# First chunk of an embedding tower: rows of eight fields by one-hot products from whole tables instead of gathers

## Chip, cores, metric

The kernel runs on one core of one Trainium2 chip. The metric is the device time of one execution, in microseconds. All arithmetic is in float32.

## What is computed

A batch of 512 rows has 32 id fields. Each id picks a row of 64 numbers from its field's table. For each of the 496 pairs of fields, a 64x64 matrix stands between the two rows, and each pair gives one number. These 496 numbers and 16 dense ones go through three dense layers.

```python
e = jnp.stack([tbl_0[ids[:, 0]], ..., tbl_31[ids[:, 31]]], axis=1)   # 512 x 32 x 64
p, q = e[:, ids_x, :], e[:, ids_y, :]                                # all pairs x < y, 496
z = einsum('bpj,bpj->bp', einsum('bpi,pij->bpj', p, w), q)           # w: 496 x 64 x 64
h = jnp.concatenate([z, dense_ctx], axis=1)                          # 512 x 512
h = jnp.maximum(h @ W_top1 + b_top1, 0.0)                            # 512
h = jnp.maximum(h @ W_top2 + b_top2, 0.0)                            # 256
y = h @ W_top3                                                       # 512 x 1
```

Twelve of the tables have 1,000 rows; the others have 1,250, 12,500 or 125,000.

## The kernel before

The batch is cut into four chunks of 128 rows. GpSimd gathers, chunk by chunk and field by field, 128 rows of 64 numbers into `emb` (L313). Two neighbouring fields make a pair `k` of 128 numbers; TensorE turns a pair over by products with `identity` (L491) into a slot of `pu`, and ScalarE copies it to `eT` (L332), where the 128 numbers are partitions and the batch rows are columns. Chunk 0 is turned pair by pair (`XN[0]` is 1), later chunks four pairs at a time.

The pair products of a chunk are 32 units. A unit is 1024 columns of `pu`, two banks of 512. There are two ways to make one.

- A **turned** unit (16 of 32, list `TURNED`) has batch rows as partitions: two products of 512 columns (L523), one for each half of the 128 rows of `eT` and `ws`. VectorE multiplies it with `emb` into `turned` (L425). Then each of its 16 numbers for each batch row is a sum over 64, a row sum. A block of 16 row sums is made by ScalarE (16 instructions, L342), by VectorE (one reduction, L451) or by GpSimd (halving six times, L299 and L302), as the table `ROWS` says, and lands in `zB`. TensorE turns `zB` (L511, for the last chunk L506) into `zT`.
- A **summed** unit has batch rows as columns: eight products of 128 columns (L531). VectorE multiplies it with `eT` into `prod` (L443, L439), and TensorE sums over partitions by four products with a column of ones in `select` into `pz` (L544).

`pu` has three slots, so TensorE can be at most three fills ahead of VectorE; `turned` has ten buffers and `prod` nine. The dense layers of a chunk (L551, L563, L573) run among the units of the next one.

The order is written out by hand in tables: `TURN_AT` (which of a chunk's 32 steps are turned units), `X_AT` (after which step each pair is turned over), `MLP_AT`, `SUMS_AT` and `ROWS`. Each engine runs its own program in that order and waits on semaphores. A step is one unit, numbered from 0 to 127 over the four chunks. A unit needs the pair `k` on its product side and four pairs from `m` on on its multiply side; units come in the order of `k`.

The start of chunk 0: SyncE loads `idx`, `identity` and the first two of eight parts of `ws` (1 MB each, L271); each later part waits for a pair of gathers (pairs 1, 3, 5, 7, 9, 11). GpSimd issues the 32 gathers of chunk 0 one behind another, and from chunk 1 on a gather for field `x` waits for step `x` of the chunk before. TensorE waits for pairs 0 to 3 before its first unit.

```python
for g in range(NU // WU):
    if g >= W_AT_ONCE:
        sp.wait_ge(s_emb[2 * (g - W_AT_ONCE) + 1], 16 * 2)
    sp.dma_start(ws[:, g * WU:(g + 1) * WU, ...], w[...]).then_inc(s_w[g], 16)
```

Of the kernel before, what the change touches and what calls it, by code (L numbers as in the profile page):

```python
# [48 lines left out]
Z_ORDER = [z for z in range(ZCH) if z >= ZA] + list(range(ZA))  # L49
assert NU == 32 and NT == 16 and all(UNITS[u][0] == "four" for u in TURNED)  # L50
assert ZCH * P == FIELDS * (FIELDS - 1) // 2 + DENSE

TURN_AT = [[2, 3, 7, 9, 10, 11, 12, 16, 17, 18, 20, 21, 22, 29, 30, 31], [5, 6, 7, 10, 11, 12, 13, 15, 18, 20, 22, 23, 25, 26, 29, 31], [2, 3, 7, 8, 9, 10, 11, 14, 17, 18, 23, 26, 27, 29, 30, 31], [0, 5, 6, 10, 11, 12, 13, 14, 15, 16, 17, 18, 19, 20, 24, 26]]
ORDER = []
# [6 lines left out]

ROWS = [[('act', 4), ('act', 7), ('dve', 7), ('dve', 9), ('act', 12), ('act', 15), ('dve', 17), ('dve', 26), ('act', 16), ('dve', 33), ('act', 20), ('act', 27), ('act', 29), ('act', 30), ('act', 35), ('act', 36)], [('act', 40), ('dve', 39), ('act', 43), ('dve', 45), ('dve', 52), ('act', 44), ('act', 50), ('act', 51), ('act', 56), ('dve', 56), ('act', 57), ('dve', 66), ('act', 61), ('dve', 69), ('act', 64), ('act', 64)], [('act', 72), ('act', 75), ('dve', 71), ('dve', 73), ('act', 75), ('act', 78), ('act', 80), ('act', 81), ('pool', 28), ('dve', 89), ('pool', 30), ('act', 94), ('act', 95), ('dve', 98), ('act', 100), ('dve', 100)], [('pool', None), ('act', 106), ('pool', None), ('act', 107), ('act', 111), ('pool', None), ('pool', None), ('dve', 112), ('pool', None), ('pool', None), ('dve', 119), ('pool', None), ('act', 121), ('dve', 123), ('act', 125), ('pool', None)]]

# [44 lines left out]
UR = 3  # L108
# [4 lines left out]
WU = 4  # L113
W_AT_ONCE = 2

XN = [1, 4, 4, 4]
GROUPS = [(c, k, XN[c]) for c in range(BCH) for k in range(0, KP, XN[c])]
NG = len(GROUPS)  # L120
# [6 lines left out]
MLP_AT = [(7, 15, 27, 37, 54), (8, 9, 34, 38, 45), (14, 15, 19, 23, 27)]  # L127
X_STEPS = [at for of_chunk in X_AT for at in of_chunk]
# [32 lines left out]

Z_LATE = [2, 1, 1, 116]
Z_OUT = [Z_LATE[c] + min(t for t in SUMS if (c + 1) * NA - 1 in SUMS[t]) for c in range(BCH - 1)]


def dlrm_tower(nc, tables, ids, w, dense, w1, b1, w2, b2, w3, ident, out):
    with ExitStack() as ctx:
# [235 lines left out]
        def _(dve):  # L403
# [73 lines left out]
        def _(pe):  # L477
# [196 lines left out]
```

## Time and profile before

| | us |
|---|---|
| median of 3 runs | 218.34 (218.11 to 218.46) |
| the profiled execution, its own time | 218.69 |
| its span, first to last instruction | 216.9 |
| TensorE busy | 191.2 (88%) |
| VectorE busy | 172.7 (80%) |
| ScalarE busy | 153.7 (71%) |
| GpSimd busy | 153.7 (71%) |

The profile comes from one execution. Its 1.8 us beside the span lie before the first and behind the last instruction. Busy time is summed for each engine; a product's row ends when its result is out, so a row of TensorE can hold waiting too. GpSimd's rows are the issuing of gathers for the most part: 121.2 of its 153.7 us. The slices are 5.4 us each.

### The profile page before, as it was taken

Reading aid. Unit: us, or ns where it says so; the run is one execution under the profiler, and the core shown is the slowest. Engines: PE = TensorE matmul, PEld = TensorE weight load, DVE = VectorE, ACT = ScalarE, POOL = GpSimd, SP = SyncE. Lnnn points to the kernel's source line nnn. Section 1 sums busy time; section 2 is a strip of 40 time slices with the busy share of each in tenths; the row PEclk is TensorE's granted clock in tenths of the full one; section 3 lists DMA queues with packets and bytes.
Section 4 is the critical chain, followed back from the end, with each engine's and each line's share of the span. In section 5 each row is a group of like instructions: output and inputs, shape, how many; then the busy total and the mean of one; then the engine's idle time right before and its main releaser. Section 6 shows DMA issues by size and latency. Waiting matters only on the chain.

```text
span 216.9 us, 6361 instructions
## 1 busy us (share of the span) xinstructions
PE 191.2 (88%) x2142; PEld 130.4 (60%) x2142; DVE 172.7 (80%) x157; ACT 153.7 (71%) x1178; POOL 153.7 (71%) x192
## 2 busy tenths in 40 slices
PE   0119869989998989999999999999999999999985
PEld 0017446534765654875876756675587745687874
DVE  0004686898999979999997999899999966999811
ACT  2000267599999989999989679997798883619401
POOL 4777777777777777777777777777788878885200
PEclk9999997999999999999999999999999999999999
DMA  5676657557111111111111111111100000000000
GB/s 186 255 228 232 233 193 237 201 168 282 27 30 29 27 30 26 27 33 26 24 34 29 24 30 28 29 30 27 26 21 14 9 2 0 3 2 3 5 0 0
DMA packets 6434, 15.23 MB, mean 70 GB/s; under 512 B 2689, under 2 KB 2945, under 8 KB 5250
## 3 DMA queue, kind: packets, MB, share of 16 engines
q1 hardware_dynamic: 2306, 10.62, 13.6%
q0 software_dynamic: 4096, 4.20, 9.3%
q8 instruction: 17, 0.28, 0.5%
q14 instruction: 15, 0.12, 0.2%
HBM read 14.82 MB, written 0.00 MB: 68 GB/s over the span
## 4 chain that ended last, share of the span: by engine, by line
PE 68%; POOL 8%; DVE 8%; issue 6%; ACT 4%; DMA 3%; DVEq 0%
PE pu L531 23%; PE pu L523 22%; PE pz L544 11%; POOL emb L313 8%; PE pt L551 5%; ACT turned L342 4%; DVE turned L425 3%; DVE prod L443 3%; PE pt L563 2%; DMA emb<-in_tbl,idx 2%; PE pu L551 1%; DVE prod L439 1%; DVE zB L451 1%; PE pu L491 1%; PE pt L573 1%
## 5 line engine op out<-in xcount | busy, mean ns | idle before, releaser
L313 POOL DMA_INDIRECT emb<-in_tbl,idx x128 | 121.2, 947 | 41.2 <-issue 29.8
L342 ACT ACTIVATE turned<-turned 128x64 f32<-128x64 f32 x560 | 134.0, 245 | 1.8 <-DVE turned L425 1.8
L342 ACT ACTIVATION_READ_ACCUMULATOR turned<-turned 128x1 f32 x560 | 107.3, 192 | 0.0
L425 DVE TENSOR_TENSOR turned<-pu,emb 128x1024 f32<-128x1024 f32 x64 | 76.0, 1217 | 9.8 <-PE pu L523 9.8
L443 DVE TENSOR_TENSOR prod<-pu,eT 128x1024 f32<-128x1024 f32 x48 | 57.1, 1217 | 22.7 <-PE pu L531 22.5
L531 PEld LDWEIGHTS pu<-eT,ws 64*128 64x128 f32 x1024 | 64.3, 193 | 16.6 <-issue 11.6
L531 PE MATMUL pu<-eT,ws 64*128 64x128 f32 x1024 | 68.7, 283 | 4.0 <-ACT eT L332 1.7
L523 PE MATMUL pu<-ws,eT 64*128 64x512 f32 x256 | 67.7, 630 | 2.4 <-DVE prod L443 0.8
L523 PEld LDWEIGHTS pu<-ws,eT 64*128 64x128 f32 x256 | 22.5, 192 | 21.5 <-issue 20.1
L332 ACT COPY eT<-pu 128x128 f32<-128x128 f32 (+1 forms) x28 | 11.1, 398 | 34.1 <-PE pu L491 34.0
L299 POOL TENSOR_TENSOR turned<-turned 128x512 f32<-128x512 f32 (+4 forms) x50 | 30.3, 607 | 6.6 <-DVE turned L425 3.3
L544 PE MATMUL pz<-prod,select 128*32 128x256 f32 x512 | 31.9, 383 | 0.0
L491 PE MATMUL pu<-identity,emb 64*128 64x64 f32 x128 | 9.5, 234 | 16.2 <-DMA emb<-in_tbl,idx 16.0
L544 PEld LDWEIGHTS pz<-prod,select 128*32 128x32 f32 x512 | 14.9, 109 | 14.4 <-DVE prod L443 2.3
L451 DVE TENSOR_REDUCE zB<-turned 128x16 f32<-128x1024 f32 x19 | 23.0, 1210 | 0.1
L491 PEld LDWEIGHTS pu<-identity,emb 64*128 64x128 f32 x128 | 7.5, 144 | 23.4 <-issue 11.7
L439 DVE TENSOR_TENSOR prod<-pu,eT 128x1024 f32<-128x1024 f32 x16 | 19.5, 1217 | 1.4 <-PE pu L531 1.4
L551 PEld LDWEIGHTS pt<-zT,w1s 128*128 128x128 f32 x104 | 12.2, 191 | 4.7 <-issue 3.4
L551 PE MATMUL pt<-zT,w1s 128*128 128x128 f32 x104 | 13.7, 283 | 0.6 <-DVE zT L457 0.6
L361 ACT ACTIVATE h<-pt,b1s 128x128 f32<-128x128 f32 x13 | 4.1, 359 | 9.7 <-PE pu L551 5.8
L370 ACT ACTIVATE h<-pt,b2s 128x128 f32<-128x128 f32 x7 | 2.2, 361 | 8.7 <-PE pt L563 6.3
L563 PE MATMUL pt<-h,w2s 128*128 128x128 f32 x56 | 7.4, 284 | 0.0
(27 smaller groups left out, 29.7 us busy)
## 6 DMA issues: line engine op xcount, KB each, us to landing
ws<-in_w SPq DMA_DIRECT2D x8, 1024.0 KB, 4.8
emb<-in_tbl,idx POOLq DMA_INDIRECT x128, 2.4
w1s<-in_w SPq DMA_DIRECT2D x1, 1024.0 KB
zT<-in_dense SPq DMA_DIRECT2D x1, 512.0 KB, 3.3
w2s<-in_w SPq DMA_DIRECT2D x1, 512.0 KB
idx<-in_ids SPq DMA_DIRECT2D x1, 64.0 KB, 2.0
identity<-in_ident SPq DMA_DIRECT2D x1, 64.0 KB, 1.9
w3s<-in_w SPq DMA_DIRECT2D x1, 1.0 KB
```

The source lines that it names most:

```text
L299: nc.gpsimd.tensor_tensor(t[:, :, 0:n], t[:, :, 0:n], t[:, :, n:2 * n], ALU.add).then_inc(halved, 1)
L313: nc.gpsimd.indirect_dma_start(out=emb[:, c % EC, x, :], out_offset=None, in_=tables[x], in_offset=bass.IndirectOffsetOnAxis(ap=idx[:, c, ...
L342: i = nc.scalar.activation(t, t, ACT.Copy, accum_out=zB[:, b // NT % 2, b % NT * 16 + v:b % NT * 16 + v + 1])
L425: nc.vector.tensor_tensor(turned[:, b % RB, :, :].rearrange("p (x f) i -> p x (f i)", x=2), u.rearrange("p x s i -> p x (s i)"), e, ALU.mu ...
L439: nc.vector.tensor_tensor(p.rearrange("p x (h s) b -> p x h (s b)", h=2), u.rearrange("p x (h s) b -> p x h (s b)", h=2), e, ALU.mult).the ...
L443: nc.vector.tensor_tensor(p.rearrange("p x s b -> p x (s b)"), u.rearrange("p x s b -> p x (s b)"), e, ALU.mult).then_inc(mult_done, 1)
L451: nc.vector.tensor_reduce(zB[:, b // NT % 2, b % NT * 16:b % NT * 16 + 16], turned[:, b % RB, :, :], axis=AXIS.X, op=ALU.add).then_inc(row ...
L491: mm = nc.tensor.transpose(to[:, i, h, :], emb[rows, c % EC, 2 * (k + i):2 * (k + i) + 2, :] .rearrange("p f e -> p (f e)"), identity[rows ...
L523: i = nc.tensor.matmul(pu[:, FILL["u", t] % UR, bank, :, :], eT[rows, c % EC, UNITS[u][1], :], ws[rows, u, :, :], start=True, stop=True)
L531: i = nc.tensor.matmul(pu[:, FILL["u", t] % UR, bank, slot, :], ws[rows, u, slot, :], eT[rows, c % EC, k, :], start=True, stop=True)
L544: mm = nc.tensor.matmul(pz[32 * g:32 * g + 32, :, :], select[:, 30 - 2 * i:62 - 2 * i], prod[:, a % PR, bank, 2 * turn:2 * turn + 2, :], s ...
L551: i = nc.tensor.matmul(l1_out(c, n), w1s[:, z, n * P:(n + 1) * P], zT[:, z, cols(c)], start=(z == Z_ORDER[0]), stop=(z == Z_ORDER[-1]))
```

## The change

Eight fields with tables of 1,000 rows (1, 3, 7, 14, 15, 19, 20, 26) are put at places 8 to 15 of the order of fields, as pairs 4 to 7; `FIELD_AT` holds the new order, and the weights, ids and tables follow it. In chunk 0 these eight are not gathered. Instead:

- SyncE loads the eight whole tables, 1,000 rows as 125 partitions of 8 rows, into parts of `turned`, 0.256 MB each; the 1,024 ids of these fields, repeated on 125 partitions (0.512 MB), into a part of `prod`; and the numbers of the rows on each partition into `rows_at`. `identity` now comes behind the fourth table.
- VectorE compares, for each of the eight fields, ids with row numbers (125x1024): a one where they are equal.
- TensorE multiplies: for each pair 16 products (8 row groups for each of two fields, each to its own half of the partitions of `pu`), summed in place. The result is the turned pair, which ScalarE copies to `eT`. It needs no gather and no turning over.

The tables of 1,000 rows stay in use by ordinary gathers in chunks 1 to 3. Places 8 to 15 have no `emb` in chunk 0, so no turned unit may multiply with them: `TURNED` is another list of 16. All order tables are other ones too. `ROWS` gives ScalarE 38 blocks instead of 35, VectorE 17 instead of 19, GpSimd 9 instead of 10. The parts 2 to 7 of `ws` wait for pairs 1, 3, 8, 9, 10, 11.

```diff
+HOT_FIELDS = (1, 3, 7, 14, 15, 19, 20, 26)
+HOT_ROWS = 1000
+HP, HJ = 125, 8
+HOT = range(8, 16)
+_REST = [f for f in range(FIELDS) if f not in HOT_FIELDS]
+FIELD_AT = _REST[:8] + list(HOT_FIELDS) + _REST[8:]
...
-TURNED = [2, 3, 5, 9, 10, 11, 12, 13, 18, 19, 20, 21, 22, 26, 28, 29]
+TURNED = [2, 3, 4, 5, 8, 10, 12, 14, 18, 20, 21, 23, 24, 26, 27, 29]
...
+W_BEHIND = (1, 3, 8, 9, 10, 11)
...
+FIRST = (4, 5, 0, 1, 6, 7, 2, 3)
+GROUPS = [(0, k, 1) for k in FIRST + tuple(range(8, KP))]
+GROUPS += [(c, k, XN[c]) for c in range(1, BCH) for k in range(0, KP, XN[c])]
...
-X_AT = [[-1, -1, -1, -1, 1, 2, 3, 4, 6, 7, 10, 12, 15, 16, 19, 24], [28, 33, 39, 48], [60, 61, 71, 74], [91, 92, 98, 109]]
+X_AT = [[-1, -1, -1, -1, -1, -1, -1, -1, 0, 5, 7, 9, 11, 13, 17, 20], [27, 31, 38, 45], [54, 63, 67, 80], [83, 93, 103, 109]]
...
+        def hot_table(i):
+            return turned[0:HP, 6 + i // 2, 8 * (i % 2):8 * (i % 2) + HJ, :]
+
+        def hot_columns(i):
+            return prod[0:HP, 5 + i % 4, :, :, :].rearrange("p x s b -> p (x s b)")
...
             sp.dma_start(idx[:], ids).then_inc(s_idx, 16)
-            sp.dma_start(identity[:], ident).then_inc(s_ident, 16)
+            sp.dma_start(hot_list(), hot_ids.broadcast_to([HP, len(HOT) * P])).then_inc(s_hot_ids, 16)
+            sp.dma_start(rows_at[0:HP, :], hot_rows).then_inc(s_hot_rows, 16)
+            for i, x in enumerate(HOT):
+                sp.dma_start(hot_table(i), tables[x].rearrange("(p j) e -> p j e", j=HJ)).then_inc(s_hot[i // 2], 16)
+                if i == 3:
+                    sp.dma_start(identity[:], ident).then_inc(s_ident, 16)
...
-                    sp.wait_ge(s_emb[2 * (g - W_AT_ONCE) + 1], 16 * 2)
+                    sp.wait_ge(s_emb[W_BEHIND[g - W_AT_ONCE]], 16 * 2)
...
+                    if is_hot(c, x // 2):
+                        continue
...
+            dve.wait_ge(s_hot_ids, 16)
+            dve.wait_ge(s_hot_rows, 16)
+            for i in range(len(HOT)):
+                if i >= 4:
+
+                    dve.wait_ge(xt_ready, hot_group(i - 4) + 1)
+                at = rows_at[0:HP, :]
+                nc.vector.tensor_tensor(hot_columns(i).rearrange("p (j b) -> p j b", j=HJ),
...
+                if is_hot(c, k):
+                    i = 2 * k - HOT[0]
+                    pe.wait_ge(ones_ready, i + 2)
+                    pe.wait_ge(s_hot[i // 2], 16 * 2)
+                    for j in range(HJ):
+                        for h in range(2):
+                            mm = nc.tensor.matmul(pu[EMB * h:EMB * (h + 1), FILL["x", g] % UR, 0, 0, :], hot_table(i + h)[:, j, :],
+                                                  hot_columns(i + h)[:, j * P:(j + 1) * P], start=(j == 0), stop=(j == HJ - 1))
+                    mm.then_inc(xt_ready, 1)
+                    return
```

SyncE's queue from the program's start, before and then changed; `idx` holds the ids for the gathers, `turned<-in_tbl` are the tables:

```order
L265 DMA idx<-in_ids 128x128
L266 DMA identity<-in_ident 128x128
L271 DMA ws<-in_w 128x2048 x8
L275 DMA zT<-in_dense 128x1024
L276 DMA w1s<-in_w 128x2048
```

```order
L304 DMA idx<-in_ids 128x128
L305 DMA prod<-in_hot_ids 125x1024
L306 DMA rows_at<-in_hot_rows 125x8
L308 DMA turned<-in_tbl 125x512 x4
L310 DMA identity<-in_ident 128x128
L308 DMA turned<-in_tbl 125x512 x4
L315 DMA ws<-in_w 128x2048 x8
```

Ten loads with 125 partitions now stand between `idx` and `ws`, and `identity` stands behind six of them.

TensorE's first rows, before and then changed; L491 and L562 turn pairs over, L553 are the table products, L531 and L602 summed units, L523 and L594 turned ones:

```order
L491 MATMUL pu<-identity,emb 128x64 x8
L531 MATMUL pu<-eT,ws 128x128 x16
L491 MATMUL pu<-identity,emb 128x64 x2
L523 MATMUL pu<-ws,eT 128x512 x2
L491 MATMUL pu<-identity,emb 128x64 x2
L523 MATMUL pu<-ws,eT 128x512 x2
```

```order
L553 MATMUL pu<-prod,turned 64x128 x32
L562 MATMUL pu<-identity,emb 128x64 x4
L553 MATMUL pu<-prod,turned 64x128 x32
L562 MATMUL pu<-identity,emb 128x64 x4
L594 MATMUL pu<-ws,eT 128x512 x2
L562 MATMUL pu<-identity,emb 128x64 x2
```

All eight pairs 0 to 7 now come ahead of the first unit, where four did; between two later units stands one pair.

VectorE's rows ahead of and behind its first multiply, changed:

```order
L515 TENSOR_TENSOR prod<-prod,rows_at 125x1024 x8
L474 TENSOR_TENSOR turned<-pu,emb 128x1024
L492 TENSOR_TENSOR prod<-pu,eT 128x1024
L474 TENSOR_TENSOR turned<-pu,emb 128x1024
L488 TENSOR_TENSOR prod<-pu,eT 128x1024
```

The eight comparisons are new; the first unit is now a turned one.

## Rows read from the trace of the kernel before

**Rows 1.** The page, part 2: busy tenths of 40 slices, clock, DMA share.

```profile
DVE  0004686898999979999997999899999966999811
...
PEclk9999997999999999999999999999999999999999
DMA  5676657557111111111111111111100000000000
```

**Rows 2.** Stretches: length, busy us of PE, PEld, DVE, ACT, POOL; clock, DMA, GB/s.

```profile
18.00:40.00 22.00, 18.74 (x172) 11.56 (x172) 16.15 (x14) 9.39 (x71) 16.68 (x18) 0.92 0.66 223
40.00:60.00 20.00, 17.92 (x208) 11.44 (x205) 18.59 (x17) 18.94 (x156) 15.12 (x17) 1.00 0.47 156
60.00:100.00 40.00, 38.12 (x466) 25.10 (x463) 38.08 (x35) 38.54 (x306) 30.24 (x33) 1.00 0.15 28
100.00:150.00 50.00, 49.46 (x596) 34.64 (x596) 47.56 (x43) 45.63 (x361) 37.81 (x41) 1.00 0.14 28
150.00:206.00 56.00, 55.80 (x627) 38.51 (x618) 50.36 (x45) 37.61 (x280) 42.14 (x71) 1.00 0.04 9
```

**Rows 3.** Timeline, 0 to 30 us: start, us, engine, line, [idle before].

```profile
2.99 1.09 POOL L313 DMA_INDIRECT emb<-in_tbl,idx  x1 [2.54 <-DMA idx<-in_ids]
4.39 0.94 POOL L313 DMA_INDIRECT emb<-in_tbl,idx  x1 [0.30 <-issue]
...
9.71 0.61 PE L491 MATMUL pu<-identity,emb 64*128 64x64 f32 x4 [9.71 <-DMA emb<-in_tbl,idx]
...
15.29 0.37 PE L491 MATMUL pu<-identity,emb 64*128 64x64 f32 x2 [0.99 <-DMA emb<-in_tbl,idx]
...
16.06 3.79 PE L531 MATMUL pu<-eT,ws 64*128 64x128 f32 x32 [0.40 <-ACT eT L332]
...
18.18 1.23 DVE L443 TENSOR_TENSOR prod<-pu,eT 128x1024 f32<-128x1024 f32 x1 [17.01 <-PE pu L531]
...
20.35 1.97 PE L523 MATMUL pu<-ws,eT 64*128 64x512 f32 x4 [0.40 <-issue]
...
22.77 1.13 PE L523 MATMUL pu<-ws,eT 64*128 64x512 f32 x4 [0.40 <-issue]
```

**Rows 4.** A stretch of 1 us under the first load of ws, columns as in rows 2.

```profile
4.00:5.00 1.00, 0.00 (x0) 0.00 (x0) 0.00 (x0) 0.00 (x0) 0.69 (x2) 1.00 0.99 418
```

**Rows 5.** The page, parts 3 and 6: GpSimd's gathers.

```profile
q0 software_dynamic: 4096, 4.20, 9.3%
...
emb<-in_tbl,idx POOLq DMA_INDIRECT x128, 2.4
```

**Rows 6.** Timeline of TensorE, at full speed.

```profile
80.04 2.06 PE L531 MATMUL pu<-eT,ws 64*128 64x128 f32 x32 [1.05 <-DVE turned L425]
...
83.74 1.07 PE L544 MATMUL pz<-prod,select 128*32 128x256 f32 x16
...
88.41 2.05 PE L551 MATMUL pt<-zT,w1s 128*128 128x128 f32 x16
...
172.16 2.80 PE L544 MATMUL pz<-prod,select 128*32 128x256 f32 x48
```

**Rows 7.** Timeline of VectorE, back to back.

```profile
102.06 1.21 DVE L443 TENSOR_TENSOR prod<-pu,eT 128x1024 f32<-128x1024 f32 x1
103.19 1.21 DVE L451 TENSOR_REDUCE zB<-turned 128x16 f32<-128x1024 f32 x1
```

**Rows 8.** Timeline of ScalarE: two row sums, thirty starts apart.

```profile
62.41 0.24 ACT L342 ACTIVATE turned<-turned 128x64 f32<-128x64 f32 x1
...
69.57 0.24 ACT L342 ACTIVATE turned<-turned 128x64 f32<-128x64 f32 x1
```

**Rows 9.** Timeline of VectorE: a late stall and the last product.

```profile
176.07 3.49 DVE L425 TENSOR_TENSOR turned<-pu,emb 128x1024 f32<-128x1024 f32 x3 [1.82 <-PE pu L523]
...
205.11 1.21 DVE L439 TENSOR_TENSOR prod<-pu,eT 128x1024 f32<-128x1024 f32 x1
```

**Rows 10.** A stretch of 1 us, columns as in rows 2.

```profile
34.00:35.00 1.00, 1.00 (x4) 0.41 (x2) 1.00 (x1) 1.00 (x11) 0.70 (x2) 0.50 0.97 410
```

More of the change, by code:

```diff
@@ L32, with is_hot @@
 KP = FIELDS // 2
+HOT_FIELDS = (1, 3, 7, 14, 15, 19, 20, 26)
+HOT_ROWS = 1000
+HP, HJ = 125, 8
+assert HP * HJ == HOT_ROWS
+HOT = range(8, 16)
+_REST = [f for f in range(FIELDS) if f not in HOT_FIELDS]
+FIELD_AT = _REST[:8] + list(HOT_FIELDS) + _REST[8:]
+def is_hot(c, k):
+    return c == 0 and 2 * k in HOT
 UNITS = []
@@ L50 @@
 assert NU == 32 and NT == 16 and all(UNITS[u][0] == "four" for u in TURNED)
+assert all(2 * (UNITS[u][2] + i) not in HOT for u in TURNED for i in range(4))
 assert ZCH * P == FIELDS * (FIELDS - 1) // 2 + DENSE
-TURN_AT = [[2, 3, 7, 9, 10, 11, 12, 16, 17, 18, 20, 21, 22, 29, 30, 31], [5, 6, 7, 10, 11, 12, 13, 15, 18, 20, 22, 23, 25, 26, 29, 31], [2, 3, 7, 8, 9, 10, 11, 14, 17, 18, 23, 26, 27, 29, 30, 31], [0, 5, 6, 10, 11, 12, 13, 14, 15, 16, 17, 18, 19, 20, 24, 26]]
+TURN_AT = [[0, 2, 4, 6, 8, 9, 10, 13, 14, 17, 19, 21, 24, 27, 30, 31], [4, 5, 6, 7, 11, 14, 16, 17, 18, 20, 21, 22, 25, 29, 30, 31], [2, 6, 7, 9, 12, 13, 15, 17, 18, 19, 21, 22, 23, 25, 26, 30], [1, 4, 5, 6, 9, 10, 11, 14, 18, 19, 20, 22, 23, 25, 26, 27]]
 ORDER = []
@@ L114 @@
 W_AT_ONCE = 2
+W_BEHIND = (1, 3, 8, 9, 10, 11)
 XN = [1, 4, 4, 4]
-GROUPS = [(c, k, XN[c]) for c in range(BCH) for k in range(0, KP, XN[c])]
+FIRST = (4, 5, 0, 1, 6, 7, 2, 3)
+assert XN[0] == 1
+GROUPS = [(0, k, 1) for k in FIRST + tuple(range(8, KP))]
+GROUPS += [(c, k, XN[c]) for c in range(1, BCH) for k in range(0, KP, XN[c])]
 NG = len(GROUPS)
-X_AT = [[-1, -1, -1, -1, 1, 2, 3, 4, 6, 7, 10, 12, 15, 16, 19, 24], [28, 33, 39, 48], [60, 61, 71, 74], [91, 92, 98, 109]]
-MLP_AT = [(7, 15, 27, 37, 54), (8, 9, 34, 38, 45), (14, 15, 19, 23, 27)]
+X_AT = [[-1, -1, -1, -1, -1, -1, -1, -1, 0, 5, 7, 9, 11, 13, 17, 20], [27, 31, 38, 45], [54, 63, 67, 80], [83, 93, 103, 109]]
+MLP_AT = [(14, 19, 26, 39, 51), (13, 16, 22, 29, 36), (10, 13, 17, 21, 25)]
 X_STEPS = [at for of_chunk in X_AT for at in of_chunk]
@@ L160, with dlrm_tower @@
 SUMS[NS] = list(range(_a, BCH * NA))
-Z_LATE = [2, 1, 1, 116]
+Z_LATE = [3, 1, 4, 291]
 Z_OUT = [Z_LATE[c] + min(t for t in SUMS if (c + 1) * NA - 1 in SUMS[t]) for c in range(BCH - 1)]
-def dlrm_tower(nc, tables, ids, w, dense, w1, b1, w2, b2, w3, ident, out):
+def dlrm_tower(nc, tables, ids, hot_ids, hot_rows, w, dense, w1, b1, w2, b2, w3, ident, out):
     with ExitStack() as ctx:
@@ L175, in sem @@
             return ctx.enter_context(nc.semaphore(name))
+        rows_at = sb("rows_at", [P, HJ], I32)
         idx = sb("idx", [P, BCH, FIELDS], I32)
@@ L202, in dlrm_tower @@
         s_emb = [sem(f"emb_in{i}") for i in range(BCH * KP)]
+        s_hot_ids = sem("hot_ids_in")
+        s_hot_rows = sem("hot_rows_in")
+        s_hot = [sem(f"hot_tables_in{i}") for i in range(len(HOT) // 2)]
+        ones_ready = sem("ones_ready")
         s_w = [sem(f"w_in{i}") for i in range(NU // WU)]
@@ L250, in turned_over, with hot_list, hot_group @@
                 .rearrange("p h (i b) -> p i h b", b=BH)
+        def hot_table(i):
+            return turned[0:HP, 6 + i // 2, 8 * (i % 2):8 * (i % 2) + HJ, :]
+        def hot_columns(i):
+            return prod[0:HP, 5 + i % 4, :, :, :].rearrange("p x s b -> p (x s b)")
+        def hot_list():
+            return prod[0:HP, 4, :, :, :].rearrange("p x s b -> p (x s b)").bitcast(I32)
+        def hot_group(i):
+            return GROUP_OF[0, HOT[i] // 2]
         def slot_free(engine, fill):
@@ L485, in transpose_x @@
                 slot_free(pe, ("x", g))
+                if is_hot(c, k):
+                    i = 2 * k - HOT[0]
[6 more added lines that the diff above has]
+                    mm.then_inc(xt_ready, 1)
+                    return
                 to = turned_over(("x", g), n)
@@ L639 @@
                         continue
-                    x, y = 2 * k + bank, 2 * m + r
+                    x, y = FIELD_AT[2 * k + bank], FIELD_AT[2 * m + r]
                     block = w[pair[min(x, y), max(x, y)]]
@@ L650 @@
     arrays = {
-        "ids": np.asarray(inputs["ids"]).reshape(BCH, P, FIELDS).transpose(1, 0, 2),
+        "hot_ids": np.asarray(inputs["ids"])[:P, list(HOT_FIELDS)].T.reshape(1, len(HOT) * P),
+        "hot_rows": np.arange(HOT_ROWS, dtype=np.int32).reshape(HP, HJ),
+        "ids": np.asarray(inputs["ids"])[:, FIELD_AT].reshape(BCH, P, FIELDS).transpose(1, 0, 2),
         "w": w_blocks.reshape(P, NU, 4, P),
@@ L668 @@
     out = nc.dram_tensor("out_y", (BATCH, 1), F32, kind="ExternalOutput").ap()
-    dlrm_tower(nc, [aps[f"tbl_{f}"] for f in range(FIELDS)], aps["ids"], aps["w"], aps["dense"],
+    dlrm_tower(nc, [aps[f"tbl_{f}"] for f in FIELD_AT], aps["ids"], aps["hot_ids"], aps["hot_rows"], aps["w"], aps["dense"],
                aps["w1"], aps["b1"], aps["w2"], aps["b2"], aps["w3"], aps["ident"],
```

9 lines of the change are left out of this document (7 added, 2 removed).

## Prediction

> **What bounds the kernel now.** I read the page's slices first [rows 1]: VectorE is idle for three slices (5.4 us each), only half to four fifths busy for five more, and then nearly full until slice 38. The stretches say the same in us [rows 2]: from its first product to 40 us VectorE is busy 16.15 us, which leaves 5.7 idle, then 1.4 in 40 to 60, 1.9 in 60 to 100, 2.4 in 100 to 150 and 5.6 in 150 to 206. Of the 188 us between 18.18 and the end of its last product at 206.3 [rows 3, 9] it works 171, 1.16 us for each of 147 operations. So VectorE's work sets the time, plus the moment it starts, its few idle us, and the 10.6 us behind its last product. TensorE reads busier in rows 2, but its rows stretch while it waits for a free slot of pu. By full-speed rows [rows 6] a unit of eight products takes half of 2.06 us, less than the 1.13 from one VectorE operation to the next [rows 7]. It comes close to a bound only where sums and the dense layers bunch, as before the 1.82 us stall of [rows 9].
>
> The timeline of the start [rows 3] says why VectorE begins at 18.18 and then starves. GpSimd issues one gather each 1.25 us from 2.99 on. A field pair needs two, so a row group k of eT can come each 2.5 us; k=3 is turned at 15.29 and the first products run at 16.06. Pairs feed few units at first, so VectorE waits until about 40 us. Those are the two things that the change addresses: the pace of gathers, and what can run before they land.
>
> **The change, part by part.**
>
> *Gathers.* Eight of the 32 gathers of chunk 0 go. The last of the chunk is then issued 8 x 1.25 = 10 us earlier (from 42.7 to 32.7). Pairs 0 to 3 still need the first eight gathers, landing as before at about 15.3 [rows 3]. Pairs 4 to 7 need none. So as soon as the first unit can run, eight units are open, and pairs 8, 9, 10, 11 follow each 2.5 us from about 18 to 26, while ten units wait on each two to four of them. VectorE needs about 1.25 us per unit, so gathers no longer starve it. I take the idle rate of the stretch 60 to 100 (1.9 in 40 us) for the first 42 us: 2.0 instead of 5.7 + 1.4 = 7.1, **-5.1 us**. The bounds are 0 gained (the handoffs that starve it are PE's) and 7.1.
>
> *Comparisons on VectorE.* Eight of 125x1024, nearest row the reduction over 1024 from SBUF, 1.21 us, 1.13 apart [rows 7]: 9.0 us. They stand ahead of the first multiply, where VectorE idled 17.01 us [rows 3], and that covers them: they cost nothing by themselves. But comparisons 4 and 5 wait until TensorE is done with the first table group, 6 and 7 for the second, so a late TensorE delays them, and they the fourth group.
>
> *Table products on TensorE.* Four groups of 16 products, 128 columns each. Two go to different halves of the columns. Products on different column groups run side by side: 16 records of L544 with 256 columns take 1.07 us, while 16 of L551, full width and 128 columns, take 2.05 [rows 6]. So a group costs about as much as two units of L531, 32 records: 2.06 us at full speed, 3.79 as the first ones of before did [rows 3, 6]. One after the other would be twice that, my upper bound. Rows 3 show the same records at half speed from 16.06 until past 20.35 (1.97 against 1.13 at 22.77), after an engine that had stood nearly idle; PEclk reads 1.00 there [rows 1], so the durations tell it and that column doesn't. I give the first group 3.8, the second 3, the last two 1.9.
>
> *Loads on SyncE's queue.* This decides. Ahead of the 2 MB of ws now stand 0.51 MB of ids written to 125 partitions, and eight tables of 0.256 MB, also 125 partitions: 2.56 MB. With all sixteen DMA engines (share 0.99) 418 GB/s move [rows 4], and the first gather starts at 2.99 because its ids have landed, so bytes flow from about 2.4. Everything up to table 7, 2.7 MB, would be in by 2.4 + 2.7/0.42 = 8.8 us, ws's first part by 11.3. But each load of before has 128 rows, eight for each engine. 125 is 5 x 5 x 5: sixteen engines can't share it equally, nor can any number up to sixteen except five. No row shows a load of 125. So the bounds are sixteen engines at 418 GB/s and five at 5/16 of it, 131 GB/s. I take five, since equal shares are the only dealing that the rows show. Then the tables need 2.56/0.131 = 19.5 us. Gathers share these engines: q0's 128 gathers took 9.3% of the span [rows 5], 0.158 us each on every engine, 2.4 us for fifteen. Table 7 lands at 2.4 + 19.5 + 2.4 = 24.3, table 3 at about 15, identity (issued behind table 3, and the first thing TensorE waits for) with it. The first part of ws has 64 KB for each engine, 2.5 us, and more gathers go beside it: 27.3. Parts 1 to 7 follow 2.5 us apart, from 29.8, on the five engines; units need them at steps 4, 8, 10, 14, 17, 24 and 26, of 1.25 us each, the nearest at 33.6. The new gates (pairs 1, 3, 8, 9, 10, 11 for 1, 3, 5, 7, 9, 11) open early enough, and dense and the layer weights, gated by pair 15, go 10 us earlier: no cost.
>
> The Trainium skill bears on this: "DMA: Bandwidth & Descriptors", section "Why a DMA increments its semaphore by 16 and not by 1", says the number of engines is the largest up to sixteen that divides the slowest dimension of both sides, so five for 125. No row here has such a load. By that rule the sum is the one with five engines below, and without it the one with sixteen.
>
> *The chain to the first multiply, with five.* TensorE starts at 15; first table group to 18.8; second to 21.8; comparisons 6 and 7 by 24.1; pairs 0 and 1; third group to 24.3; fourth to 26.3; pairs 2 and 3 and their copies to 27. The first unit needs ws at 27.3, gives u at 28.4, and VectorE multiplies at **28.6**: 10.4 us later than 18.18. *With sixteen* the start is TensorE's: 7.0 (identity and two comparisons), 10.8, 13.8, pairs 0 and 1 at 14.4, third group to 16.5, fourth to 18.5, pairs 2 and 3 to 19.1, first u 20.1, multiply at 20.3: +2.1 us.
>
> *Row sums.* The table of who sums rows has 17 reductions on VectorE instead of 19: 2 x 1.13 = **-2.3 us**. ScalarE gets 38 blocks instead of 35, GpSimd 9 instead of 10. A block is 16 of L342; thirty lie between the two of [rows 8], 7.16 us, so a block is 3.8 us and ScalarE gains 11.5. It has 50 - 45.6 and 56 - 37.6 us free late [rows 2], but in 60 to 100 only 1.5. From 30 us on it can do chunk 0's 13 blocks and its copies by about 83. They are needed where z of chunk 0 is turned, at step 46: 28.6 + 49 operations x 1.16 + 2.5 idle = 88. Chunk 1's eleven are done by about 130 and needed at step 77, 86 operations on, at 133. So the extra blocks are hidden, with 3 to 5 us to spare.
>
> *Other turned units and orders.* As many units of each kind, so equal work. The stalls of 100 to 206 (8.1 us together) may grow or shrink by 3; in chunk 3 seven sums now stand in one place (3 us of TensorE) where six gave 1.82 of stall [rows 6, 9]. I take 0. Last leftovers are two sums in both, so the 10.6 us behind the last product stay.
>
> *Sum*: +10.4 - 2.3 - 5.1 = **+3.0 us** on the profiled execution's 218.69, 221.7; that execution lies 0.35 above the median 218.34, so 221.3 on that scale.
>
> **The rivals.**
> *A, the other side: all sixteen engines carry the 125-row loads.* Then +2.1 - 2.3 - 5.1 = -5.3: 213.0. It decides if table 7 lands before about 16 us; the break-even is a first multiply at 25.6. For it: engines share bytes evenly in all that the rows show, and 8.8 us is early enough to be hidden. Against: it needs unequal shares. Chance 0.30.
> *B, my forecast.* 0.58. Its own range is 218.5 to 224.5: per-engine speed for 2 KB rows and gathers beside it move the start between 26 and 30.5, later stalls by 1.5.
> *C: gathers get held up too.* Under the 2 MB load of before the second gather, issued at 4.39, was not used until 9.71, 5.3 us later [rows 3], against 2.4 in the median [rows 5]. With five engines loaded to 29 us pairs 8 to 11 would come 3 us late besides: 224. Chance 0.06.
> *D: sixteen engines, but the table products run one after the other, or ScalarE's extra blocks stall z of chunk 1.* 3 to 5 us of A's gain go: 217. Chance 0.06.
> That the change doesn't do what it says can be left out: the order shows the gathers gone. GpSimd's later gathers wait for units (gather x of chunk 1 for unit x), and with a late start they follow it; each is used 13 or more steps on, so that costs nothing. One more thing could help in every case: the granted clock fell to 0.50 [rows 10] around 34 us, its lower level of 1.2 GHz, in the stretch where TensorE still waited for gathers now and then; without those waits it may not fall. That is part of the 5.7 us above.
>
> **How the numbers follow.** A measurement of this kernel can tell about 0.2%, 0.44 us. Faster: all of A (0.30), 0.05 of B, 0.04 of D: 0.39. Slower: 0.49 of B, 0.06 of C, 0.01 of D: 0.56. Within: 0.05. The range must hold both A and B, since neither has 0.8: from 212.0 (A with a us of luck) to 224.5 (B's end).
>
> **What would show it.** The gap between issue and landing of the table loads: 2 to 6 us right away for A, growing to about 19 for the last one in B, with the DMA share in 5 to 20 us near 0.4 instead of 0.8 and above. TensorE's first table product at about 15 (B) or 7 (A). VectorE's first multiply at 28.6 or 20.3, idle between it and 40 us under 2 us, 17 reductions. If it starts late and the whole is still faster, the later stalls have shrunk, and my 0 for the orders is the wrong term. If it starts early and nothing is gained, TensorE or ScalarE bounds, and it's the reading of VectorE as the limit that fails.

## The result, and the profile after

The changed kernel takes **226.04 us** (median of 4 runs, 225.39 to 226.74), the kernel before 218.38 us beside it: ratio 1.035, 95% interval 1.032 to 1.039. It is 7.7 us slower; forecast were 221.3 us with a range from 212.0 to 224.5. The profiled execution took 226.48 us, its span is 224.6.

The page's slices of the changed kernel, part 2, and below them the bytes moved before:

```profile
DVE  0523404989999998999999899989999987989921
...
PEclk9999958999999999999999999999999999999999
DMA  4649999994210111111011110011001000000000
GB/s 84 136 143 278 262 346 396 398 350 149 68 30 23 33 26 27 26 28 24 23 28 23 28 23 4 18 28 27 16 23 35 6 3 3 0 1 3 0 3 2
```

```profile
GB/s 186 255 228 232 233 193 237 201 168 282 27 30 29 27 30 26 27 33 26 24 34 29 24 30 28 29 30 27 26 21 14 9 2 0 3 2 3 5 0 0
```

Each slice is 5.6 us (5.4 before). VectorE is not full before the eighth, and the DMA engines move 84, 136 and 143 GB/s in the first three, where they moved 186, 255 and 228. The timeline of the start, three engines one after the other (start, us, engine, line, [idle before]):

```profile
4.83 2.80 SPq L310 DMA_DIRECT2D identity<-in_ident  x1
7.67 6.57 SPq L308 DMA_DIRECT2D turned<-in_tbl  x4
14.29 5.70 SPq L315 DMA_DIRECT2D ws<-in_w  x4
...
16.78 6.33 PE L553 MATMUL pu<-prod,turned 125*64 125x128 f32 x64 [16.78 <-DMA identity<-in_ident]
23.04 0.34 PE L562 MATMUL pu<-identity,emb 64*128 64x64 f32 x4
23.75 1.97 PE L553 MATMUL pu<-prod,turned 125*64 125x128 f32 x32 [0.37 <-ACT eT L381]
30.70 3.68 PE L553 MATMUL pu<-prod,turned 125*64 125x128 f32 x32 [4.99 <-DMA turned<-in_tbl]
34.31 0.48 PE L562 MATMUL pu<-identity,emb 64*128 64x64 f32 x4
34.83 1.60 PE L594 MATMUL pu<-ws,eT 64*128 64x512 f32 x4
...
7.90 4.68 DVE L515 TENSOR_TENSOR prod<-prod,rows_at 125x1024 f32<-125x1024 int32 x4 [6.73 <-DMA rows_at<-in_hot_rows]
20.50 2.36 DVE L515 TENSOR_TENSOR prod<-prod,rows_at 125x1024 f32<-125x1024 int32 x2 [7.92 <-PE pu L553]
23.16 2.36 DVE L515 TENSOR_TENSOR prod<-prod,rows_at 125x1024 f32<-125x1024 int32 x2 [0.29 <-PE pu L553]
36.47 1.23 DVE L474 TENSOR_TENSOR turned<-pu,emb 128x1024 f32<-128x1024 f32 x1 [10.95 <-PE pu L594]
```

VectorE's first multiply is at 36.47, where it was at 18.18 [rows 3]: 18.3 us later. TensorE gets to its first two groups at 16.78, when identity lands. It stands 4.99 us for the last table, which is in by 30.70 (its last packet ended at 29.7), and then does the fourth group in 3.68 us, the same 32 records that took 1.97 a moment before. Its clock, by stretches (length, busy us of PE, PEld, DVE, ACT, POOL; clock, DMA share, GB/s):

```profile
25.00:30.00 5.00, 0.71 (x14) 0.47 (x9) 0.52 (x1) 0.27 (x1) 3.78 (x5) 0.90 1.04 268
30.00:35.00 5.00, 4.26 (x38) 3.80 (x40) 0.00 (x0) 0.54 (x3) 3.78 (x5) 0.50 1.01 381
35.00:40.00 5.00, 4.59 (x44) 3.15 (x46) 3.34 (x3) 2.69 (x21) 2.82 (x4) 0.92 1.02 399
```

The granted clock fell while TensorE stood, and it is 0.50, its lower level of 1.2 GHz, for the fourth group and most of the first unit. The chain that ended last says it too (start, us, what):

```profile
4.83 2.80 SPq L310
8.78 4.09 SPq L308
12.91 17.66 DMA turned<-in_tbl
30.70 3.68 PE pu L553 x32
```

The last table is issued at 12.91 and is under way for 17.66 us; SyncE itself had stood 4.09 us in one issue before it. Behind the first multiply, VectorE's stretches (length, busy us, clock, DMA share, GB/s), of the changed kernel and then of the kernel before (its first stretch, and the sum of its four; the first stretch holds 33 operations here and 30 there):

```profile
36.47:76.00 39.53, 37.75 (x33) 1.00 0.48 176
76.00:116.00 40.00, 38.13 (x35) 1.00 0.11 26
116.00:164.00 48.00, 45.64 (x41) 1.00 0.09 21
164.00:214.51 50.51, 46.37 (x42) 1.00 0.03 8
```

```profile
18.18:60.00 41.82, 34.73 (x30) 0.96 0.57 190
...
sum 188.12, DVE 171.04; mean DVE 42.76
```

Now VectorE works 167.9 of 178.0 us, before 171.0 of 188.1. So the 7.7 us of span come as: first multiply +18.3; VectorE's work -3.2; its idle in the first stretch 7.1 to 1.8, -5.3; its idle in the rest 10.0 to 8.4, -1.6; behind the last product 10.6 to 10.1, -0.5. How the idle time falls into the first stretch and the rest depends on where I cut; its total, 17.1 to 10.2, doesn't.

### The profile page after: what moved, and what is told of

It reads as the page before. It is cut to its first block, busy times and chain, and to the rows that moved or that the text cites. A ratio compares the mean times of both kernels' runs of the same rounds, so it can differ in the third digit from the quotient of the medians.

```text
span 224.6 us, 6707 instructions
## 1 busy us (share of the span) xinstructions
PE 197.9 (88%) x2262; PEld 137.8 (61%) x2262; DVE 178.9 (80%) x163; ACT 164.4 (73%) x1274; POOL 145.4 (65%) x178
## 3 DMA queue, kind: packets, MB, share of 16 engines
q1 hardware_dynamic: 3606, 13.19, 17.1%
## 4 chain that ended last, share of the span: by engine, by line
PE 81%; DMA 8%; SPq 5%; DVE 3%; issue 1%; ACT 0%; DVEq 0%
PE pu L602 27%; PE pu L594 26%; PE pz L615 14%; DMA turned<-in_tbl 8%; PE pt L622 6%; SPq L308 3%; PE pt L634 3%; DVE turned L474 2%; PE pu L553 2%; PE pu L562 1%; SPq L310 1%; PE pu L622 1%; DVE prod L492 1%; PE pt L644 1%; PE pu L634 0%
## 5 line engine op out<-in xcount | busy, mean ns | idle before, releaser
L391 ACT ACTIVATE turned<-turned 128x64 f32<-128x64 f32 x608 | 145.5, 244 | 0.9 <-DVE turned L474 0.9
L359 POOL DMA_INDIRECT emb<-in_tbl,idx x120 | 116.0, 966 | 46.3 <-issue 22.6
L391 ACT ACTIVATION_READ_ACCUMULATOR turned<-turned 128x1 f32 x608 | 115.8, 190 | 0.0
L602 PEld LDWEIGHTS pu<-eT,ws 64*128 64x128 f32 x1024 | 62.4, 188 | 19.0 <-issue 16.9
L602 PE MATMUL pu<-eT,ws 64*128 64x128 f32 x1024 | 67.2, 277 | 0.8 <-DVE turned L474 0.7
L594 PE MATMUL pu<-ws,eT 64*128 64x512 f32 x256 | 66.0, 614 | 0.7 <-DVE turned L474 0.4
L343 POOL TENSOR_TENSOR turned<-turned 128x512 f32<-128x512 f32 (+4 forms) x45 | 27.3, 607 | 17.7 <-DVE turned L474 14.8
L594 PEld LDWEIGHTS pu<-ws,eT 64*128 64x128 f32 x256 | 21.8, 188 | 16.4 <-issue 14.5
L553 PE MATMUL pu<-prod,turned 125*64 125x128 f32 x128 | 12.0, 368 | 22.1 <-DMA identity<-in_ident 16.8
L553 PEld LDWEIGHTS pu<-prod,turned 125*64 125x64 f32 x128 | 11.2, 195 | 22.5 <-DMA identity<-in_ident 16.8
L515 DVE TENSOR_TENSOR prod<-prod,rows_at 125x1024 f32<-125x1024 int32 x8 | 9.4, 1224 | 14.9 <-PE pu L553 8.2
L500 DVE TENSOR_REDUCE zB<-turned 128x16 f32<-128x1024 f32 x17 | 20.5, 1209 | 0.1
```

The source lines that it names most:

```text
L343: nc.gpsimd.tensor_tensor(t[:, :, 0:n], t[:, :, 0:n], t[:, :, n:2 * n], ALU.add).then_inc(halved, 1)
L359: nc.gpsimd.indirect_dma_start(out=emb[:, c % EC, x, :], out_offset=None, in_=tables[x], in_offset=bass.IndirectOffsetOnAxis(ap=idx[:, c, ...
L391: i = nc.scalar.activation(t, t, ACT.Copy, accum_out=zB[:, b // NT % 2, b % NT * 16 + v:b % NT * 16 + v + 1])
L500: nc.vector.tensor_reduce(zB[:, b // NT % 2, b % NT * 16:b % NT * 16 + 16], turned[:, b % RB, :, :], axis=AXIS.X, op=ALU.add).then_inc(row ...
L553: mm = nc.tensor.matmul(pu[EMB * h:EMB * (h + 1), FILL["x", g] % UR, 0, 0, :], hot_table(i + h)[:, j, :], hot_columns(i + h)[:, j * P:(j + ...
L594: i = nc.tensor.matmul(pu[:, FILL["u", t] % UR, bank, :, :], eT[rows, c % EC, UNITS[u][1], :], ws[rows, u, :, :], start=True, stop=True)
```

## The experiments

The first eight runs fell in a time in which TensorE stood for long in every kernel: the kernel before took 264 to 267 us there. Their totals can tell little, and only their landings are used. All later runs had the kernel before at 218.7 to 219.05 us. It shows in the waits of the kernel before itself, run unchanged as e7_before (engine, line waited for: us, times, longest):

```profile
PEld pu L523 <- issue: 52.2, 49, 29.8
```

It took 265.83 us in its one run, with the first multiply at 22.2. "issue" means that no engine and no DMA in the trace ended the wait. That TensorE waited for instructions is my guess, and not shown: in the longest gap, 19.8 to 49.3 us, the trace has no load on an instruction queue. For short I call TensorE held up where this happens.

> The kernel before itself, for its trace on the chips where it takes 264 us. If the extra 46 us are TensorE waiting for instructions, its trace shows idle time before TensorE that no engine or DMA ends, 30 us and more in all; VectorE's idle time grows by as much. If the chip is one on which it takes 218.4, its trace is that of the first profile.

**Loads dealt to all sixteen engines (e1_even; e4, e5, e8 again).** Each table is loaded as two pieces, 112 rows (7 for each of sixteen engines) and 13; ids and row numbers go to 128 partitions.

```diff
-sp.dma_start(hot_list(), hot_ids.broadcast_to([HP, len(HOT) * P]))
-sp.dma_start(rows_at[0:HP, :], hot_rows)
+sp.dma_start(prod[:, 4, ...], hot_ids.broadcast_to([P, len(HOT) * P]))
+sp.dma_start(rows_at[:], hot_rows)
 for i, x in enumerate(HOT):
-    sp.dma_start(hot_table(i), rows)
+    sp.dma_start(hot_table(i)[0:112], rows[0:112])
+    sp.dma_start(hot_table(i)[112:HP], rows[112:HP])
...
-pe.wait_ge(s_hot[i // 2], 16 * 2)
+pe.wait_ge(s_hot[i // 2], 16 * 4)
```

> The changed kernel with the same bytes of tables, but dealt evenly: each table as a load of 112 rows and one of 13, and ids and row numbers on 128 partitions. Theory T (a load of 125 rows is carried by five of the sixteen DMA engines, so everything behind it waits): the last table lands by about 12 us instead of 30.6, the first multiply comes at 20 to 22 us instead of 36.5, and the time falls by 14 to 16 us, to 210 to 212. Rival R (it is the 2.6 MB more ahead of ws, however they are dealt): the last table still lands after 25 us and the time stays above 222. Rival O (the other orders and the move of row sums make it slow): the first multiply comes early, but the stretch from it to the last product, 178.1 us in the changed kernel, grows by what the start gains.

Measured 267.65 us beside 265.59 (ratio 1.011, 1.001 to 1.022); the repeats gave 263.02 to 268.09 beside 261.54 to 267.67 (e4), 265.32 beside 264.05 and 268.19 beside 266.97. The kernel of e11 below ran here too (e6_ident): 264.62 beside 264.05, its first table product at 9.03. In e1 the first table product came at 10.35 instead of 16.78, and the last 2 KB packet of a table was through at 13.6 instead of 29.7; then TensorE was held up, and the first multiply came at 41.4, where 20 to 22 were expected. The landings speak for theory T and against R; time and first multiply missed it, and by themselves say nothing.

**The dose (e3_dose).** Tables and ids in pieces of 100 rows and of 25:

```diff
-    sp.dma_start(hot_table(i), rows)
+    sp.dma_start(hot_table(i)[0:100], rows[0:100])
+    sp.dma_start(hot_table(i)[100:HP], rows[100:HP])
```

> The changed kernel with tables and ids as loads of 100 and 25 rows. By theory T 100 rows are dealt to ten engines and 25 to five, so the busiest engine carries 15 rows of each where it carried 25, and 8 in the even version. The tables' own time then falls to 15/25: the last table lands at about 17 to 20 us and the first multiply comes at 22 to 26, between the even version and the changed kernel; time 212 to 217. If the number of engines does not matter (rival R), it lands as in the changed kernel, or later for the 9 loads more that SyncE issues: time above 224.

Identity landed at 13.32, between 10.35 (112 and 13) and 16.78 (125), and the last table packet was through at 20.5, between 13.6 and 29.7; 271.26 us beside 265.59, with TensorE held up and the first multiply at 46.1. 100 rows can be dealt evenly to ten engines at most, 125 to five, 112 to sixteen, and the landings come in that order.

**The same, with TensorE not held up (e9_after, e10_even_beside, e11_ident_beside; one chip, 3 rounds).** e9 is the changed kernel, e10 the kernel of e1, e11 issues row numbers, ids and identity ahead of the even tables:

```diff
+sp.dma_start(rows_at[:], hot_rows)
 sp.dma_start(prod[:, 4, ...], hot_ids.broadcast_to([P, len(HOT) * P]))
-sp.dma_start(rows_at[:], hot_rows)
+sp.dma_start(identity[:], ident)
 for i, x in enumerate(HOT):
...
-    if i == 3:
-        sp.dma_start(identity[:], ident)
```

> The changed kernel itself, beside the kernel before on this chip. Earlier runs had the kernel before at 264 to 267 us, with TensorE standing for instructions for 10 to 30 us after the first products; if this chip does so too, the 8 us of the change should be partly covered by that wait: theory (late tables) expects 1.02 to 1.035, with identity landed at 16.8 us and the last table at 30.6; if this chip doesn't, 1.035. Rival (the loss lies in later work): landings may be as before and the loss the same.

> The same with each table loaded as rows 0:112 and 112:125, and ids and row numbers on 128 partitions. Theory (late tables): 2 to 3% below the changed kernel on the same chip, its first table product at about 10.4 us against 16.8 and pairs 0 and 1 at about 17; the third group without the 5 us wait. Rival (loads' landing is covered by other work): the same time as the changed kernel.

> The even loads with row numbers, ids and identity issued ahead of the tables. Theory: another 1 to 2 us below the even loads, first table product at 9.0 us. Rival: no difference, since the first multiply waits for the last table or for instructions.

```text
kernel                 median us  range            ratio to before (95%)
before                 219.05     217.77 - 219.60
e9  changed            225.99     225.40 - 226.62  1.033 (1.028 - 1.037)
e10 even loads         213.65     213.08 - 214.14  0.975 (0.971 - 0.979)
e11 even, identity 1st 214.17     212.44 - 215.92  0.981 (0.975 - 0.987)
```

This is the main result: **dealing the same loads to all engines takes 12.3 us off** (their bytes are equal to 0.01 MB of 13.2), and the change then beats the kernel before by 2.5%. The page of e10 and its timeline, TensorE and then VectorE:

```profile
GB/s 138 265 303 400 394 394 354 217 240 28 27 32 27 28 28 32 25 27 29 32 27 28 27 26 14 25 34 17 19 32 23 3 0 3 0 2 3 0 3 2
```

```profile
11.40 6.64 PE L555 MATMUL pu<-prod,turned 125*64 125x128 f32 x64 [11.40 <-DMA identity<-in_ident]
...
18.40 1.97 PE L555 MATMUL pu<-prod,turned 125*64 125x128 f32 x32
...
20.55 1.97 PE L555 MATMUL pu<-prod,turned 125*64 125x128 f32 x32 [0.18 <-issue]
...
24.13 1.23 DVE L476 TENSOR_TENSOR turned<-pu,emb 128x1024 f32<-128x1024 f32 x1 [3.68 <-PE pu L596]
```

265 and 303 GB/s stand where 136 and 143 stood; groups three and four follow with at most 0.18 us between and at full clock; the first multiply comes 12.34 us earlier than at 36.47, and the span is 212.3, 12.3 us shorter. From the first multiply to the end it is 188.2 us here and 188.1 in the changed kernel. That answers rival O of e1: the stretch does not grow by what the start gains.

**ws held back until the tables are in (e2_gate, e12_gate).** One added line ahead of the loads of ws, the 125-row loads left as they are:

```diff
+sp.wait_ge(s_hot[3], 16 * 2)
 for g in range(NU // WU):
```

> The changed kernel with one wait more: SyncE issues ws only when the last table is in. Theory W (once ws is issued at 14.3 us its packets share the five engines with the tables that are still queued, so the last table lands at 30.6 instead of the forecast 24.3): the last table lands at 23 to 25 us; ws's first part then needs about 5 us more, the first multiply comes at about 30 and the time falls by some 6 us to 220. Rival G (gathers or slow 2 KB rows are what made it 30.6): the last table lands at 29 to 31 as before, the first multiply moves to about 37 and the time does not fall.

> The changed kernel, but the loads of ws are issued only once table 7 has landed. Theory (ws's packets share the five engines with the last tables): table 7 lands 5 us earlier, at 25.6 instead of 30.6 us, while the first part of ws comes at about 28.5; so the first multiply is at about 30 to 31 us instead of 36.5 and the kernel takes 5 to 6 us less than 226, about 220.5. Rival (the last tables are late by themselves, or the later parts of ws then stall the units): the first multiply comes early but the time stays within 2 us of 226.

With TensorE held up (e2): 271.67 us beside 265.59, but the last table was in at 25.6. In e12: **221.61 us** (221.34 to 222.78) beside 218.9, ratio 1.015 (1.011 to 1.019), 4.4 us less than the changed kernel (5 to 6 were expected). SyncE's issue of ws, TensorE's fourth group and its wait for ws, VectorE's first multiply:

```profile
25.42 4.15 SPq L316 DMA_DIRECT2D ws<-in_w  x8
...
25.75 1.97 PE L554 MATMUL pu<-prod,turned 125*64 125x128 f32 x32 [0.18 <-DVE prod L516]
...
30.24 1.13 PE L595 MATMUL pu<-ws,eT 64*128 64x512 f32 x4 [2.25 <-DMA ws<-in_w]
...
31.41 1.23 DVE L475 TENSOR_TENSOR turned<-pu,emb 128x1024 f32<-128x1024 f32 x1 [5.76 <-PE pu L595]
```

The last table is in at 25.4 at the latest (the issue that waits for it starts then), not at 30.7: the loads of ws had cost it 5 us. The fourth group takes 1.97 us: TensorE had stood for only 0.18 us before it. The first multiply is 5.06 us earlier, the span 5.0 (219.6).

How ws costs the tables 5 us the gate alone can't tell, but the lengths of single DMA packets in the traces can: 2 KB for the tables, 8 KB for ws. Between 18 and 24 us:

```text
                         2 KB, us each  engines busy with 2 KB   8 KB, us each  engines busy with 8 KB
changed kernel           0.140          4.8                      0.480          10.9
e9, the same kernel      0.139          4.8                      0.468          10.9
e12, ws held back        0.086          4.9                      -              0
```

Before ws's first packet, in 10 to 14 us, a packet of the changed kernel takes 0.084 us too. So the five engines of the tables carry tables all the time, in both kernels, and ws runs on the eleven others; what ws changes is the length of every packet. The first part of ws bears it out, in the view of issues at 14.2 us (name, issues, KB, us to landing):

```profile
ws<-in_w SPq DMA_DIRECT2D x1, 1024.0 KB, 19.2
```

It lands at 33.5. The last table packet ends at 29.7, and eight packets of 8 KB, ws's share on each of the five engines, take about 3 us more (an estimate from 0.33 us each, as in 31.5 to 40 us). What the engines share that makes them slower side by side is not shown.

**The other two terms (e13 to e17).** e13 and e14 put one table of before back into the even kernel, e15 is that kernel beside them; e16 gives two sums of rows back to VectorE, beside e17, the even kernel, and e18, the kernel of e11 (5 rounds):

```diff
 ROWS = [...]           # e13: the whole table as before
 SUMS_AT = (...)        # e14: the whole table as before
-('act', 63), ..., ('act', 97)    # e16: one in chunk 1, one in chunk 2
+('dve', 54), ..., ('dve', 88)
```

> Even loads, with the table of who sums which rows as before the change (19 reductions on VectorE, 35 blocks on ScalarE, 10 on GpSimd). Theory (each reduction costs its time on VectorE): 2.3 to 2.5 us more than the even loads. Rival (the table's places matter, not its count): over 4 us more, by stalls where a sum now comes before its rows are there. Second rival: no difference, because the saved time is idle elsewhere.

> Even loads, with the places of TensorE's sums (SUMS_AT) as before the change. The prediction put the orders at 0 with bounds of 3 us either way. Theory (orders are worth nothing by themselves): within 1 us of the even loads. Rival (they're worth about 1 to 3 us in shorter stalls after 100 us): 1 to 3 us slower.

> Even loads, with two of ScalarE's sums of rows (one in chunk 1, one in chunk 2) given back to VectorE at the step at which they are ready, everything else as it is: 19 reductions instead of 17. Theory (VectorE's work sets the time, 1.13 to 1.21 us each): 2.3 to 2.4 us more than the even loads. Rival (VectorE has idle time to take them, since TensorE or ScalarE is the limit): under 1 us more.

> Even loads with identity, ids and row numbers ahead of the tables; the first multiply came 3.1 us earlier than with the even loads (21.01 against 24.13), the medians were 214.2 and 213.65. Theory (a start earlier is worth its full length): 2 to 3 us less than the even loads. Rival (the earlier start is given back while the next pairs' gathers are waited for, since those do not come earlier): within 1 us.

```text
kernel                 median us  range            ratio to before (95%)
e13 row sums of before 246.93     246.13 - 247.94  1.131 (1.126 - 1.135)
e14 sums of before     224.50     224.11 - 224.65  1.026 (1.023 - 1.029)
e15 even loads         213.44     213.05 - 215.27  0.979 (0.974 - 0.984)
e16 two sums back      215.08     214.82 - 215.44  0.985 (0.982 - 0.988)
e17 even loads         213.55     212.74 - 214.33  0.977 (0.974 - 0.981)
e18 even, identity 1st 214.88     213.28 - 215.83  0.983 (0.979 - 0.987)
```

e13 costs 33 us and e14 11 us more than e15. In e13 VectorE's longest wait is this one:

```profile
99.17 1.22 DVE L490 TENSOR_TENSOR prod<-pu,eT 128x1024 f32<-128x1024 f32 x1 [6.69 <-PE pu L604]
```

And in its waits TensorE has this row, and the even kernel has none such (us, times, longest):

```profile
PE pu L604 <- ACT eT L383: 13.9, 6, 6.4
```

TensorE waits for ScalarE's copies, which stand behind sums of rows placed for another order. Each table fits its own order of units, so a table from elsewhere tells of the misfit, not of what the order is worth. In e13 that was the first rival; e14 missed both its theory and its rival (1 to 3 us), and the waits of e14 were not followed up. The term "orders" stays untested by itself. The full set, all tables of before with the hot fields, was not run.

e16 is the clean one: 1.5 us more than e17, where 2.3 to 2.4 were expected. Run against run on the same chip the means differ by 1.6 us, 0.6 either way; the ratios to the kernel before, 0.0075 apart with 0.005 either way, could not rule out 2.4. VectorE is busy 2.06 us longer in the trace (180.99 against 178.93), and its waits for L604 go from 3.3 to 2.1 us, so part of the work seems to have gone into time that it had waited.

e18 is no faster than e17. Its TensorE timeline, and its clock:

```profile
21.32 0.28 PE L563 MATMUL pu<-identity,emb 64*128 64x64 f32 x2 [2.29 <-DMA emb<-in_tbl,idx]
21.45 1.78 PE L595 MATMUL pu<-ws,eT 64*128 64x512 f32 x4
24.12 0.37 PE L563 MATMUL pu<-identity,emb 64*128 64x64 f32 x2 [0.89 <-DMA emb<-in_tbl,idx]
24.25 2.07 PE L603 MATMUL pu<-eT,ws 64*128 64x128 f32 x16
```

```profile
20.00:30.00 10.00, 7.79 (x50) 4.97 (x52) 4.38 (x4) 4.35 (x34) 7.56 (x9) 0.66 1.00 380
```

The table products are ready earlier, but the gathers are not: TensorE waits for them, the clock falls to 0.66 in 20 to 30 us, and a first unit takes 1.78 us where e10's took 1.13. Its first multiply is at 23.27, and the span is 214.0. In the profiled execution of e11, the same kernel, the first multiply was at 21.01, the clock stayed at 1.00 and the span was 210.6. So the same program falls to the lower clock in some executions and not in others. The ten executions of e11 and e18 order themselves by it: spans of 210.6 to 211.8 us at a mean clock of 1.00, 212.9 to 213.1 at 0.992, 214.0 to 214.1 at 0.983 or 0.984. The even kernel has 210.9 to 212.5 at 1.00. So where the clock holds, the earlier start is worth about half a us, and e18's rival (given back in waiting for gathers) fits that; with the clock fallen the same program took 1 to 3 us more. What decides the fall stayed open.

## Why the prediction was wrong, step by step

By parts: the first multiply came 18.3 us later where +10.4 stood, and all behind it gave back 10.6 us where 7.4 stood. So the start was 7.9 us worse than forecast, and 3.2 us of that were hidden by what came out better behind it.

- **Five engines for 125 rows: right.** The step that the whole rested on. In 10 to 12 us the loads' queue takes this share:

```profile
q1 hardware_dynamic: 126, 0.24, 31.4%
```

  31.4% is 5/16, and 0.24 MB in 2 us is 120 GB/s against my 131. Rival A (sixteen engines) is out for this kernel. That its time, 213.0, is near the 213.65 of the loads dealt to sixteen is luck in part: A put table 7 at 8.8 us and the first multiply at 20.3, and they came at 14.2 (its last packet) and 24.13. On sixteen engines, all busy, the loads' queue moved 0.43 MB in 8 to 10 us and 0.53 in 10 to 12, so 215 and 265 GB/s and not 418: about twice the speed of five, not 3.2 times. Most of A's 3.8 us were made good by the 3.2 above. Five engines is what the Trainium skill's rule gives ("DMA: Bandwidth & Descriptors", section "Why a DMA increments its semaphore by 16 and not by 1"): the largest number up to sixteen that divides the slowest dimension of both sides. The trace agrees for 125, with packets that keep 5.0 engines busy in 10 to 14 us, and the landings of e3 and e1 order themselves as it says.
- **"Table 7 lands at 24.3", the failed step.** It landed at 30.7. I let the tables keep their 131 GB/s until they were in, and priced ws only behind them (27.3). On the five engines the order was so, but ws is issued from 14.29 and runs on the other eleven meanwhile, and for that the sum has no term. In 20 to 24 us the loads' queue takes nearly all sixteen engines, here and then with ws held back (e12):

```profile
q1 hardware_dynamic: 235, 0.96, 94.0%
...
q1 hardware_dynamic: 238, 0.47, 30.7%
```

  Beside ws a 2 KB packet of a table took 0.140 us, without it 0.086. e12 measured what that is worth: table in by 25.4, 1.1 us behind my 24.3, so 5 of the 6.4 us are ws's; the last one goes with the 120 GB/s in place of 131. That e12's 221.6 us lie 0.3 from my forecast is luck: its first multiply was at 31.41, 2.8 us behind my 28.6, partly since ws then came late (TensorE waited 2.25 us for it), and the 3.2 us above make up for it. TensorE's start (16.8 for 15) is not ws's doing, for it was 16.67 in e12; the loads' queue moved 0.20 and 0.18 MB in 4 to 6 and 6 to 8 us, 95 GB/s.
- **"The last two groups 1.9 each": half right.** The third took 1.97, the fourth 3.68, at a granted clock of 0.50 behind the 4.99 us of waiting for that table. The first unit at 1.60 adds half a us. I had priced the fourth after a TensorE without a gap. So the 7.9 us that the first multiply is late of 28.6 are 6.4 of the table, 1.8 of the fourth group and 0.5 of the unit, less 0.8: TensorE no longer waited for ws, and the steps between were shorter.
- **Comparisons cost nothing: right**, 9.4 us of VectorE ahead of the first multiply. The two groups of the start took 6.33 together, as my 3.8 and 3.
- **Idle 7.1 to 2.0, -5.1: right**, 7.09 to 1.78, -5.3. It holds at either start: the even kernel has the same 188 us behind a first multiply 12 us earlier. Rival C saw gathers held up, and they were: the three issued in 20 to 24 us took 8.0 us to land (median), against 2.4 over the whole. With a start this late nothing waited for them.
- **Row sums, -2.3:** VectorE's work fell by 3.2 us in the trace. The reductions are 2.5 of it (23.0 to 20.5 us); the rest I take for operations that follow one another more closely, whose rows overlap. Put back alone, two reductions cost 1.5 us (e16). So the sign is right, and there a reduction was worth less than its length.
- **Orders 0:** the later stalls shrank by 1.6 and the end by 0.5, inside the bounds of 3 that I gave.
- **The range** to 224.5 gave the start 26 to 30.5. It took the per-engine speed as the unknown, and no term for a load that is issued behind the tables and still slows them, nor for the clock. With both, and the rest as I had it, the forecast would have been about 229 (221.3 + 7.9): a right start alone would have missed by 3 us on the other side.

## What to carry to other kernels

Look at the partition count of a load that something waits for: 125 rows in one piece went at 5/16 of the bandwidth, and pieces of 112 and 13 gave 12.3 us back without a byte less. What is issued behind a load on the same queue can delay it as well, even from other engines (a wait ahead of ws gave 4.4 us), so count it in, and look for the lower clock behind the gap that the delay leaves. Of the kernels that ran, the even loads are the best (213.65, 213.44 and 213.55 us, against 219.05, 218.9 and 218.71 of the kernel before beside them).

## What I had not expected of the hardware

- DMA engines slow each other though they carry different loads: a 2 KB packet took 0.084 us with five engines at work on loads, and 0.140 with the other eleven on ws. The cause is open.
- SyncE can stand in an issue: 2.80 us for identity and 4.09 for one table while five engines carried all the loads, where these issues took 0.32 to 0.44 each in the even kernel. What it waits for inside the issue is not shown.
- TensorE at the lower level (0.50) nearly doubled the price of a group (1.97 to 3.68) just behind a wait of 4.99 us, so the late load was paid for twice.
- In some hours the same program took 264 us where it took 218 in others, on the same chip too, with TensorE standing up to 29.8 us at a time for nothing that the trace shows, behind about the same first 19 us of products. No edit of mine explains it, and I did not find its cause.
